# A planner with other priorities: the same attention, expert and scan work, issued in another order

## What is computed

```python
x = x + 0.5 * L0_ffn(layernorm(x))    # router, 8 experts, top 2, capacity, gelu(a)*g
x = x + L0_attn(layernorm(x))         # 16 heads of 8, causal, a slope per head
x = x + 0.5 * L0_ffn(layernorm(x))    # the same experts again
x = x + 0.5 * L1_ffn(layernorm(x))    # latent attention (16 heads) + 8 small experts, silu
x = x + L1_attn(layernorm(x))         # in_W, conv of 3, tanh/softplus, a scan in time, out_W, then gelu ffn
x = x + 0.5 * L1_ffn(layernorm(x))    # latent attention + small experts again
```

## Time and profile before

| what | value |
|---|---|
| median of 3 runs | 1462.42 us (1457.88 to 1463.39) |
| the profiled execution | 1457.45 us |
| its span in the trace | 1455.6 us |
| PE busy | 1343.7 us, 92% of the span |
| DVE busy | 1006.8 us, 69% |
| ACT busy | 866.9 us, 60% |
| POOL busy | 396.7 us, 27% |
| mean clock granted to PE | 0.962 of full |

### The profile page before, as it was taken

The page is one execution under the profiler, slowest core; times in us unless marked ns, Lnnn a source line. Parts: engine busy times, 40 slices in busy tenths (PEclk is TensorE's granted clock), DMA queues, the critical chain, the costliest instruction groups (busy, mean ns, idle before and its releaser), DMA issues.

```text
span 1455.6 us, 27093 instructions
## 1 busy us (share of the span) xinstructions
PE 1343.7 (92%) x10934; PEld 571.7 (39%) x10934; DVE 1006.8 (69%) x1516; ACT 866.9 (60%) x1100; POOL 396.7 (27%) x331
## 2 busy tenths in 40 slices
PE   7899998898889999989999989899988999989997
PEld 5344343333334444433444333443333444433432
DVE  3534778889815457778978757978867687766734
ACT  4344357788773562546567687566765766546672
POOL 5554420011014654522222023021232042202010
PEclk8999999999999999979999999999998999989998
DMA  6623101000005331101111010111010110101100
GB/s 173 118 58 69 33 5 44 3 2 2 2 1 109 121 68 24 26 6 23 34 24 23 1 23 1 34 24 23 1 23 1 23 34 6 26 8 23 24 1 15
DMA packets 30291, 45.80 MB, mean 31 GB/s; under 512 B 5892, under 2 KB 10692, under 8 KB 30116
## 3 DMA queue, kind: packets, MB, share of 16 engines
q1 hardware_dynamic: 30168, 44.08, 13.8%
HBM read 25.39 MB, written 1.18 MB: 18 GB/s over the span
## 4 chain that ended last, share of the span: by engine, by line
PE 76%; ACT 10%; DVE 8%; issue 5%; DMA 0%; POOL 0%; POOLq 0%; ACTq 0%; DVEq 0%; SPq 0%
PE ps L1251 14%; PE ps L1351 12%; PE ps L1296 8%; ACT PR L1429 6%; PE ps L1217 6%; PE ps L1237 5%; PE ps L1218 5%; PE ps L1219 5%; PE ps L1831 3%; DVE BM L1517 2%; PE ps L1315 2%; PE ps L1229 2%; PE ps L1258 2%; PE ps L1362 2%; PE ps L1363 1%
## 5 line engine op out<-in xcount | busy, mean ns | idle before, releaser
L1429 ACT ACTIVATE PR<-ps 128x1024 f32<-128x1024 f32 x432 | 432.4, 1025 | 220.8 <-PE ps L1258 126.2
L1517 DVE TENSOR_REDUCE BM<-ps 128x2 f32<-128x1024 f32 (+2 forms) x384 | 349.6, 951 | 48.0 <-PE ps L1237 47.4
L1251 PE MATMUL ps<-QS,KS 48*128 48x512 f16 (+7 forms) x2688 | 310.5, 333 | 46.6 <-ACT PR L1429 35.0
L1351 PE MATMUL ps<-PR,VS 128*32 128x512 f32 (+3 forms) x2304 | 234.3, 501 | 3.6 <-ACT PR L1429 3.1
L1251 PEld LDWEIGHTS ps<-QS,KS 48*128 48x128 f16 (+1 forms) x2688 | 109.9, 96 | 214.5 <-ACT PR L1429 111.1
L1237 PE MATMUL ps<-KS,QS 48*128 48x128 f16 (+2 forms) x1728 | 161.4, 274 | 15.6 <-DVE BM L1517 6.5
L1510 DVE TENSOR_REDUCE BM<-ps 128x8 f32<-128x1024 f32 x96 | 116.9, 1220 | 35.4 <-PE ps L1237 34.7
L1237 PEld LDWEIGHTS ps<-KS,QS 48*128 48x128 f16 x1728 | 69.0, 95 | 129.2 <-issue 48.0
L1217 PE MATMUL ps<-YA,QS 128*128 128x512 f16 x256 | 99.8, 390 | 1.1 <-DVE RX L1476 1.0
L1558 POOL TENSOR_TENSOR OS<-OS,RX 128x512 f32<-128x512 f32 x24 | 30.5, 1272 | 255.4 <-ACT RX L1445 255.4
L1218 PE MATMUL ps<-YA,QS 128*128 128x512 f16 x256 | 99.3, 388 | 0.0
(11 more groups left out here) (299 smaller groups left out, 2070.3 us busy)
## 6 DMA issues: line engine op xcount, KB each, us to landing
PR<-gates SPq DMA_DIRECT2D x32, 512.0 KB, 11.9
QS<-KS SPq DMA_DIRECT2D x64, 128.0 KB
QS<-KS SPq DMA_DIRECT2D x64, 64.0 KB
WM<-W_in SPq DMA_DIRECT2D x1, 2048.0 KB, 9.1
QS<-HL SPq DMA_DIRECT2D x48, 32.0 KB
KS<-HL SPq DMA_DIRECT2D x48, 32.0 KB
QS<-CT SPq DMA_DIRECT2D x96, 2.0 KB
KS<-KS SPq DMA_DIRECT2D x8, 128.0 KB, 2.4
```

Of the source, the lines that this page charges most:

```text
L1251: ins = pe.matmul(ps[pair][:, w, off:off + cols], KS[rows, ks, kt * P:(kt + 1) * P], QS[rows, qs, (ph + 1) * TT - cols:(ph + 1) * TT], sta ...
L1351: ins = pe.matmul(dst[32 * j:32 * j + 32, TT - cols:TT], v, PR[:, buf, j, off:off + cols], start=(g == 0), stop=(g == NGRP[ph] - 1))
L1429: act.activation(dst, src, ACT.Exp, scale=0.125 if lat else 1.0).then_inc(sig["exp"], 1)
L1517: ins = dve.tensor_reduce(BM[:, ph, p, :, qt - 4 * ph, part], bnk[:, :, off:off + nk * P], AX.X, ALU.max)
```

## The change

No instruction that computes is added or taken away; only the loads of ACT's function tables can change in number. Four things are edited. The constants of PE's priorities become a table, `WISH`, one for each half, with other values. `ORDER` has another sequence for ACT in both halves, for DVE and SP in the first, and for POOL in both. The planner's clock goes from event to event and no longer in steps of 0.02. `COST`, `LAND`, the streams, what each task needs, and the emitting code are untouched.

In the first half a unit that leads by three or four phases gets 2.89 in place of 2.1, `pv` 2.15 and 4.25 in place of 2.5 and 3.5, `proj` 3.84 in place of 2.7, `qk` -0.24 and `mean` -0.34 in place of 1; on ACT `exp` and `rx` come ahead of `ln`, `vln` and `sq`; on DVE `den` is last. In the second half PE's numbers move little (`pv` 3.61 and `proj` 3.06; `qk` isn't used there); on ACT `exp` comes ahead of `ge`, `dl`, `xh`, `th`, `de` and `ln`.

```diff
--- before.py
+++ after.py
@@ -117,10 +117,15 @@
     LAND = {"crow": 2.5, "put": 4.0, "egb": 2.4, "gd": 2.3, "ro": 0.0}
     TABLE = {"eg": "gelu", "rxp": "exp", "exp": "exp", "ln": "exp", "rx": "exp", "vln": "exp", "vex": "exp"}
     MODE = {"sc": 1, "un": 1, "pv": 2}
-    ORDER = {"ACT": ("rxp", "exh", "ewh", "cmc", "eg", "qkh", "vc", "ev", "sq", "vln", "vex", "ln", "exp", "rx"),
-             "DVE": ("ro", "exl", "ewl", "eup", "eh", "ct", "m4", "den", "cen", "scl", "qkl", "add", "red"),
-             "POOL": ("et", "vs", "on"),
-             "SP": ("gd", "egb", "crow", "put")}
+    ORDER = {"ACT": ("eg", "rxp", "exh", "ewh", "cmc", "vex", "qkh", "vc", "ev", "exp", "rx", "ln", "vln", "sq"),
+             "DVE": ("ro", "exl", "ewl", "eup", "cen", "eh", "scl", "ct", "m4", "add", "qkl", "red", "den"),
+             "POOL": ("vs", "et", "on"),
+             "SP": ("crow", "gd", "put", "egb")}
+
+    WISH = {"scm": 2, "unm": 2, "leadm": 4, "upm": 2, "bldm": 2, "sc": 2, "sc1": 1, "un0": 1.9, "un2": 2.89,
+            "lead": 2, "un1": 1, "une": 1, "pv3": 2.15, "ahead": 3, "pv": 4.25, "qk": -0.24, "vl": 1.91, "proj":
+            3.84, "ed": 1.1, "mean": -0.34, "eu": 1.2, "eu1": 0.3, "mode": 0.4, "bldf": 0.9, "bld2": 3.49,
+            "bld": 1.8, "up": 2.16, "dn": 1.5, "short": 1}
 
     def __init__(self):
         self.needs, self.streams, self.frees, self.room, self.at_first = {}, {}, {}, {}, {}
@@ -243,7 +248,7 @@
         return 2 * (self.at["un"][1] - self.at["sc"][1]) + self.at["un"][2] - self.at["sc"][2]
 
     def priority(self, eng, task, t):
-        kind = task[0]
+        kind, w = task[0], self.WISH
         if kind in ("ewh", "ewl") and task[1] >= E:
             return 99
         if eng == "ACT":
@@ -254,23 +259,23 @@
         if kind in ("rlg", "rrk", "rtp"):
             return 0
         if kind == "eu":
-            return 1.2 + sum(1 for x in self.held.values() if x[0] == "eu") * 0.3
+            return w["eu"] + w["eu1"] * sum(1 for x in self.held.values() if x[0] == "eu")
         scores = sum(1 for x in self.held.values() if x[0] == "sc")
         units = sum(1 for x in self.held.values() if x[0] == "un")
         if kind == "sc":
-            v = None if scores >= 2 else 2 + scores
+            v = None if scores >= w["scm"] else w["sc"] + w["sc1"] * scores
         elif kind == "un":
             lead = self.lead()
-            v = None if units >= 2 or lead > 4 else (1.9 if lead <= 2 else 2.1) + units - (self.at["eu"][1] < 63)
+            v = None if units >= w["unm"] or lead > w["leadm"] else (w["un0"] if lead <= w["lead"] else w["un2"]) + w["un1"] * units - w["une"] * (self.at["eu"][1] < 63)
         elif kind == "pv":
             e = self.at["exp"]
             ahead = group(e[1], e[2], group_of_step(e[2], e[3])) - group(*task[1:])
-            v = 2.5 if ahead >= 3 else 3.5
+            v = w["pv3"] if ahead >= w["ahead"] else w["pv"]
         else:
-            v = {"turn": 0, "qk": 1, "val": 1.9, "proj": 2.7, "ed": 1.1, "mean": 1, "var": 1}[kind]
+            v = {"turn": 0, "qk": w["qk"], "val": w["vl"], "proj": w["proj"], "ed": w["ed"], "mean": w["mean"], "var": w["mean"]}[kind]
             if kind in ("ed", "mean", "var"):
                 return v
-        return v if v is None or self.mode != self.MODE.get(kind, 3) else v - 0.4
+        return v if v is None or self.mode != self.MODE.get(kind, 3) else v - w["mode"]
 
     def extra(self, eng, task):
         if eng != "ACT":
@@ -331,21 +336,22 @@
         free = {e: 0.0 for e in engines}
         seen, self.start, back = {}, {}, {}
         left = len(self.needs)
+        pending = []
         t = 0.0
         while left:
             for s, own in list(self.held.items()):
-                if all(seen.get(x, 1e9) <= t for x in self.frees[own]):
+                if all(seen.get(x, 1e9) <= t + 1e-9 for x in self.frees[own]):
                     back[s] = max(seen[x] for x in self.frees[own])
                     del self.held[s]
             for e in engines:
-                if free[e] > t:
+                if free[e] > t + 1e-9:
                     continue
                 best = None
                 for s in of[e]:
                     if heads[s] == len(self.streams[s]):
                         continue
                     task = self.streams[s][heads[s]]
-                    if any(seen.get(x, 1e9) > t for x in self.needs[task]):
+                    if any(seen.get(x, 1e9) > t + 1e-9 for x in self.needs[task]):
                         continue
                     room = None
                     if task in self.room:
@@ -380,7 +386,9 @@
                 self.start[task] = t
                 free[e] = t + c
                 seen[task] = t + c + self.LAND.get(task[0], 0.12 if e == "PE" else 0.03)
-            t = round(t + 0.02, 2)
+                pending.append(seen[task])
+            t = min([x for x in list(free.values()) + pending if x > t + 1e-9], default=t + 1)
+            pending = [x for x in pending if x > t]
             assert t < 3000, [self.streams[s][h] for s, h in heads.items() if h < len(self.streams[s])]
         self.seen = seen
         self.count, self.total = {}, {}
@@ -458,13 +466,18 @@
     LAND = dict(Plan.LAND, wl1=4.0, wl2=3.0, kput=3.0, st=2.5)
     TABLE = {"eg": "gelu", "rxp": "exp", "si": "silu", "sg": "sigmoid", "th": "sigmoid", "ge": "gelu", "exp": "exp", "ln": "exp", "rx": "exp",
              "vln": "exp", "vex": "exp", "ve0": "exp", "rex": "exp", "de": "exp", "dl": "exp", "dx": "exp"}
-    ORDER = {"ACT": ("rxp", "exh", "ewh", "eg", "roth", "krh", "lath", "kh", "vc", "ev", "rex", "sq", "vln", "vex", "si", "xp", "sg", "th", "ab", "de",
-                     "dl", "dx", "ge", "xh", "ln", "exp", "rx", "xqh", "wqh", "ve0", "gwh"),
-             "DVE": ("ro", "exl", "ewl", "eup", "eh", "ct", "m4", "den", "cen", "scl", "scb", "rt", "gtc", "hf", "gt", "mya", "mup", "cv", "dt0", "dts", "bd",
-                     "scn", "st2", "st3", "oup", "fya", "fup", "krot", "krl", "kl", "ksw", "km", "rotd", "rotl", "swp",
-                     "bt", "latl", "cp", "add", "red", "gwl", "wql"),
-             "POOL": ("et", "psg", "pct", "pbt", "on", "xl", "ff", "rot", "xql"),
+    ORDER = {"ACT": ("rxp", "exh", "ewh", "eg", "roth", "krh", "lath", "kh", "vc", "ev", "rex", "sq", "vln", "vex",
+                     "si", "xp", "sg", "ab", "dx", "exp", "ge", "dl", "xh", "th", "de", "ln", "rx", "wqh", "xqh", "ve0",
+                     "gwh"),
+             "DVE": ("ro", "exl", "ewl", "eup", "eh", "ct", "m4", "den", "cen", "scl", "scb", "rt", "gtc", "hf", "gt",
+                     "mya", "mup", "cv", "dt0", "dts", "bd", "scn", "st2", "st3", "oup", "fya", "fup", "krot", "krl",
+                     "kl", "ksw", "km", "rotd", "rotl", "swp", "bt", "latl", "cp", "add", "red", "gwl", "wql"),
+             "POOL": ("et", "psg", "pct", "pbt", "xl", "on", "ff", "rot", "xql"),
              "SP": ("gd", "egb", "crow", "put", "kput", "st", "wl1", "wl2")}
+    WISH = {"scm": 2, "unm": 2, "leadm": 4, "upm": 2, "bldm": 2, "sc": 2, "sc1": 1.02, "un0": 1.9, "un2": 2.1,
+            "lead": 2, "un1": 1, "une": 1, "pv3": 2.5, "ahead": 3, "pv": 3.61, "qk": 0.71, "vl": 1.9, "proj":
+            3.06, "ed": 1.1, "mean": 1, "eu": 1.2, "eu1": 0.3, "mode": 0.4, "bldf": 0.8, "bld2": 3.31, "bld":
+            1.8, "up": 1.7, "dn": 1.22, "short": 1}
 
     def build(self):
         self.router()
@@ -666,13 +679,13 @@
                 m = task[1] - self.at["un"][1]
                 held = sum(1 for x in self.held.values() if x[0] == "bld")
                 first = task[1] in FAST
-                if (m > 2 and not first) or held >= (2 if first else 1):
+                if (m > w["bldm"] and not first) or held >= (2 if first else 1):
                     return None
-                return 0.8 if first else 3.2 if m > 1 or not self.began else 1.8
+                return w["bldf"] if first else w["bld2"] if m > 1 or not self.began else w["bld"]
             if kind == "up":
                 held = sum(1 for x in self.held.values() if x[0] == "up")
-                return None if held >= 2 and self.at["sc"][1] < 2 * NN - 1 else 1.7
-            return 1.5 if kind in ("dn", "val") else 1.0
+                return None if held >= w["upm"] and self.at["sc"][1] < 2 * NN - 1 else w["up"]
+            return w["dn"] if kind in ("dn", "val") else w["short"]
         if eng == "DVE" and kind in ("bt", "swp", "latl", "km", "ksw", "krot", "krl", "kl") and not self.began:
             if kind[0] != "k" and task[1] or kind[0] == "k" and task[2]:
                 return 90
```

## The result

The changed kernel took **1422.62 us** (median of four runs, 1417.40 to 1424.82) against 1461.14 (median of four too, 1457.88 to 1463.39) for the kernel before: ratio **0.9739**, interval 0.9720 to 0.9758. The sign was right; the forecast gain of 17 us is less than half of the 38.5 measured. The profiled run took 1424.82 us with a span of 1423.0. Lines of the changed kernel's Plan are shifted by 13: `exp` is L1442, its scores L1264, the units L1250, the main reductions L1530, table loads to `exp` L1886.

A forecast was written before the change was run, and what follows sets the result against it. The prediction took PE to bound the kernel, with only its idle and half-clock time to win. First half -10 and ACT's second-half list -7 gave -17 us, from 1462.4 to 1445 us, range 1424 to 1472.

The forecast's parts named there:

- PE bounds the kernel: Whole kernel: PE busy 1343.7 of 1455.6 us, so a new order gives back only its idle time and half-clock loss.
- PE's idle sum: Sign in the profile after, whole kernel: PE's idle time near 95 us, from 111.9 before.
- the forecast 18: Sign in the first half's attention: PE idle about 18 us in place of 28.5.
- Shifts starts by less than 0.02 us each: nothing.: The planner's clock by events, whole kernel: start times barely shift, so it was priced at nothing.
- The first half, -10: First-half attention: new PE numbers and ACT and DVE lists cut idle time, together -10 us (from +7 to -20).
- the story of kept units: First-half attention: units kept for later fill PE's waits for exponentials at the end, giving at most 28.5 us.
- rival A: Whole kernel: nothing measurable, the loop re-forms; first-half gain shrinks to its end, 3 us; 1460; chance 0.22.
- no long stall: First-half attention: PE's idle time is many small waits, the largest entry 13.2 us in 23 waits of 0.57 us.
- ACT's list in the second half, -7, by table loads saved: Second-half scans: exp first halves table loads, -5 us, and shortens score waits, -2 us; from +5 to -18.
- The clock, 0 plus and minus 8: Whole kernel: order may move idle pockets together or apart; value 0, bounds a sixth of the 48 us half-clock loss.
- rival C: Whole kernel: both parts reach near their bounds, -20 - 18 = -38, 1424; chance 0.10.
- Rival B: Second half: side chains come up to 29 us late each, costing 24 us in all; 1476; chance 0.18.

The follow-up runs named there:

- e1: The kernel before with only the planner's clock changed, from steps of 0.02 to going by events; ratio 0.9949.
- e6: e1 with leading units at 2.89 (`un2`) in the first half, and exp ahead of ge, dl, xh, th, de but behind ln in the second; ratio 1.0014.
- e3: The kernel before with the planner's clock by events and the new lists and numbers for the second half only; ratio 0.9836.
- e12: e1 (old lists, clock by events) with planner durations altered by up to 0.2%, seed 3; ratio 0.9886.
- e11: The changed kernel with planner durations altered by up to 0.2%, seed 3; ratio 0.9890.
- e4: The changed kernel's new lists and numbers, but with the planner's old clock in steps of 0.02; ratio 1.0061.
- e13: The kernel before (old lists, numbers and clock) with planner durations altered by up to 0.2%, seed 1; ratio 0.9899.
- e15: New lists and numbers with the planner's old clock, durations altered by up to 0.2%, seed 1; ratio 0.9935.
- e14: The kernel before (old lists, numbers and clock) with planner durations altered by up to 0.2%, seed 3; ratio 0.9898.
- e16: New lists and numbers with the planner's old clock, durations altered by up to 0.2%, seed 3; ratio 0.9898.
- e8: The changed kernel with planner durations altered by up to 0.2%, seed 1; ratio 0.9908.
- e9: The kernel before with four DVE tasks of its second half moved behind reductions that PE waits for; ratio 0.9990.
- e17: The changed kernel with second-half ACT lists and a score number altered, found by search on the planner's end, and the seed 2 noise first half; ratio 0.9828.
- e7: e1 with new ACT, DVE and SP lists but old PE numbers in the first half, and exp ahead of th alone in the second; ratio 0.9849.
- e18: The changed kernel with another second half found by search (dx behind ge, gwh ahead of ln, short 0.66), first half unchanged; ratio 0.9744.

## Why the prediction was wrong

**What holds.** PE bounds the kernel, the change can only give back PE's idle and half-clock time, and it does so with the same matmuls. PE's idle sum came to 99.2 us for the forecast 95, but that is luck: the first half was to give 10 of it and gave none (28.2 us of idle in its attention, for the forecast 18).

**"Shifts starts by less than 0.02 us each: nothing."** This step failed first. Starts shift by hundredths, but an engine takes what is ready at that moment, so a hundredth can decide which task that is, and a decision changes all that follow. e1's trace has -17.7 us in the second half and +11.0 in the first for this edit alone.

**The first half, -10.** Measured -0.6. Its end did not change: 17.39 us of `exp` in the last 34 us, and no reduction there, as in the earlier trace rows. Nothing supports the story of kept units (e6: `un2` +0.9). I took a value between the ends without a row that asked for it; rival A's 3 us was nearer. PE's waits up to 434 us also hold one of 2.5 us for the last projection, so "no long stall" was not quite so.

**ACT's list in the second half, -7, by table loads saved.** The loads rose from 78 to 82. The second half measured -34.7 whole. With the planner's clock by events in both, the half's new lists and numbers are worth 1003.9 to 984.1, -19.8 (e1 to e3), but with noise of seed 3 in both they are worth 0 (e12, e11), with the old clock +3 (before to e4), and with seeds 1 and 3 there +1.2 and -3.3 (e13 to e15, e14 to e16). The lists as such have no effect that I could show, though four pairs can't exclude one of a few us. The drop in waits for ACT, 31.0 to 10.9 us, looks like the mechanism at work, but with noise the old lists have only 16.4 to 20.4 us of them (e12 to e14) and the new ones 13.7 to 20.7 (e8, e11, e15, e16).

**The clock, 0 plus and minus 8.** This is the term that was most mis-sized: -19.9 us of PE's busy time, 60% of the gain of the span. I counted 48 us as an upper bound of the loss and then gave a sixth of it as range, without a row for the sixth. My reading that the stages at full clock are those of least idle time was loose too: in the earlier trace rows 880 to 1014 lost 7.6 of 134 us at clock 1.00, and 640 to 820 lost 8.7 of 180 at 0.98. A straight line through the 18 traces up to e16 gives the second half as 917 us + 0.94 of its idle time + 0.42 of its time at half clock, within 3.6 us. The first factor had to be near 1, since idle time is part of the length; the second is the finding. Half clock is the second currency, and it varied from 35 to 93 us.

**What took its place.** Sixteen different orders of the second half were run, not counting e9, which is the order of before but for four tasks. Ten took 1003 to 1011 us, with old and new lists and either clock. Two were slower (before 1021.6, e4 1024.7), and four faster (e17 1000.3, e7 993.3, the changed kernel's 983 to 987 in three kernels, e18 984.2). An order carries its time with it, to some 5 us: the first half of the changed kernel took 410.0, 409.3 and 410.0 in three kernels, e1's 421.6 and 423.8, e1's second half 1003.9 and 1009.4. So the change replaced an order some 14 us worse than usual by one some 20 us better than usual, and both are particular orders. My rival C had the size (1424) but the wrong mechanism, both parts near their bounds; that it came close is luck. Rival B did not happen; by its own account half of the 119 us of cover was needed for other work, so the cover was twice the delay and not four times.

**Could it have been known?** In part. The planner's own ends go from 409.5 to 402.4 for the first half and from 995.4 to 975.2 for the second, together -27.3; the prediction didn't use them. Over the sixteen orders of the second half they correlate with the chip at 0.79, with 6.9 us of scatter about the line; e17 and e18 differ by 16 us at the same plan's end. They would have been a better guide than my reading of the lists, and not a sure one.

**Left open.** Why a given order is good is not settled as a whole. Rows of units and DVE work beside POOL are places seen in traces. The longest stretch at half clock of all, 20.5 us, lies at 1122 us in e4, where seven units stand in a row. But e7's first half lost 7 us without a row, e13's second half has a row and is ordinary, and e9, which mended one pocket and moved the other, is as long as the kernel before.

## What to carry to other kernels

When a greedy planner makes the order, a change of its numbers or its clock can be little more than a new draw from a distribution of orders, and here reading what the numbers mean said little; alter its durations by a fraction of a per cent, look at the spread, and keep the best order that was measured. Before giving a change a mechanism, compare it with such a draw: here 0.2% of noise was worth 1% of the time from the kernel before (e13, e14) and up to 1.7% from the changed one (e8). And on a kernel bound by TensorE, count the time at half clock beside the idle time, since the clock can be worth more than the idle time (here 19.9 us against 12.7).

## What the runs showed of the hardware

- VectorE's `scalar_tensor_tensor` with its operands in SBUF takes far longer beside GpSimd: 128x64 0.22 us alone, and 2374 ns for the one that began with POOL's 2.33 us instruction, at 629.6; 128x1023 1.27 us alone and 3.02 beside POOL, of which 1.08 lie behind the end of POOL's instruction (1088.15 + 3.02 against 1087.64 + 2.45). The Trainium skill (SBUF — State Buffer, SBUF: two separate sides) says that of a GpSimd operation and a DVE operation with two SBUF inputs, the one that starts first gets the shared pair of ports for the whole instruction, and these times agree.
- TensorE's half clock cost about 0.4 us for each us of it (19.9 / 55.2 = 0.36 from before to after, 0.42 by the line), and not the half that a PE without idle time would lose. Part of it falls into waits, as in e13's row, where a unit of 0.39 or 0.61 us comes every 1.13 us at either clock; that this is the whole reason isn't shown.
- Waits of 0.52 us, one in each 1.13 us, went with a granted clock of 0.50 (e1, 275 to 280), while 22.4 us of idle time spread over 200 us left it at 1.00. That it matters how close together the idle time lies is read from these two cases; no run varied it alone.
